# A fused attention and expert-mixture block in split fp32: the mixture's product in two fp32r passes, with the values' read-back issued earlier

## The reference: what is computed

```python
h = layernorm(x) * (1 + ca) + sa
x = x + ga * attention(h)          # 32 heads of 128, 8 KV heads, causal, rope on 64 of 128 dims
h = layernorm(x) * (1 + cb) + sb
# experts' mixture, per token, 64 experts, top 8:
logits = h @ router_weight.T + router_bias
scores = softmax(logits); w, idx = top_k(scores, 8)
w_dense = zeros(T, 64); w_dense[token, idx] = w
out = h * w.sum() + w_dense @ expert_bias      # expert_bias is 64 x 512
x = x + gb * out
```

## Time and profile before

| | |
|---|---|
| median of 3 runs | 1534.45 us (1532.57 to 1534.9) |
| the profiled execution | 1534.65 us |
| its span | 1533.1 us |
| granted TensorE clock, mean | 0.990 |
| VectorE, ScalarE, GpSimd busy | 76%, 64%, 69% |

### The profile page before, as it was taken

One profiled execution on the slowest core, in us unless ns is written; L12 is line 12 of the kernel. 1 busy time (PEld: TensorE's weight loads), 2 busy tenths in 40 slices (PEclk: granted clock), 3 DMA queues, 4 the chain that ended last, 5 costly groups with the idle time before them and its releaser, 6 DMA issues.

```text
span 1533.1 us, 24840 instructions
## 1 busy us (share of the span) xinstructions
PE 1495.0 (98%) x7474; PEld 1260.7 (82%) x7474; DVE 1160.9 (76%) x3433; ACT 975.5 (64%) x2315; POOL 1061.0 (69%) x801
## 2 busy tenths in 40 slices
PE   7979999999999999999999999999999999999987
PEld 4668888888888888888888888888888888888875
DVE  6866777777777777778777777777878888887765
ACT  3346766677666666667667676676656666665673
POOL 1666766776667676667667667666777878876765
PEclk9999999999999999999999999999999999999996
DMA  8547565665656656566565665667678778787760
GB/s 307 212 146 234 193 216 180 202 201 185 213 184 208 202 190 212 181 206 191 194 202 190 211 198 196 202 197 230 204 242 269 258 256 263 250 264 250 242 183 28
DMA packets 210741, 321.62 MB, mean 210 GB/s; under 512 B 38368, under 2 KB 128224, under 8 KB 210608
## 3 DMA queue, kind: packets, MB, share of 16 engines
q1 hardware_dynamic: 210288, 319.94, 65.3%
q10 hardware_dynamic: 320, 0.11, 0.0%
HBM read 179.02 MB, written 140.94 MB: 209 GB/s over the span
## 4 chain that ended last, share of the span: by engine, by line
PE 82%; POOL 5%; DVE 4%; DMA 3%; SPq 2%; issue 2%; ACT 2%; POOLq 0%; DVEq 0%; ACTq 0%
PE bank_s L483 20%; PE bank_o L580 20%; PE bank_pv L565 14%; PE bank_s L530 13%; PE bank_s L506 5%; PE bank_s L494 5%; POOL PT_lo L1424 2%; PE bank_s L462 1%; PE bank_s L598 1%; DMA blocks<-blocks 1%; PE bank_s L610 1%; DMA kv_raw<-vblocks 1%; SPq L1693 1%; SPq L1656 1%; DMA wmod<-in_wmod 1%
## 5 line engine op out<-in xcount | busy, mean ns | idle before, releaser
L1424 POOL TENSOR_TENSOR PT_lo<-PT_raw,PT_hi 128x640 fp32r<-128x640 f32 x252 | 399.3, 1608 | 70.8 <-ACT PT_hi L828 70.6
L814 ACT ACTIVATE probs<-probs,row_inv 128x512 f32<-128x512 f32 (+3 forms) x512 | 258.8, 554 | 178.4 <-DVE row_inv L1105 178.0
L1412 POOL TENSOR_TENSOR rot_c<-rot_c,rot_s 128x512 f32<-128x512 f32 x128 | 165.6, 1294 | 243.5 <-DVE rot_s L1068 243.5
L807 ACT ACTIVATE probs<-probs,row_min 128x512 f32<-128x512 f32 (+3 forms) x512 | 280.6, 552 | 8.7 <-DVE row_min L1099 8.5
L1099 DVE CUSTOM_DVE_ANT_0 probs<-bank_s,mask 128x512 f32<-128x512 f32 (+3 forms) x512 | 231.5, 487 | 1.0 <-issue 0.6
L1417 POOL TENSOR_TENSOR qT_lo<-rot_c,qT_hi 128x512 fp32r<-128x512 f32 x128 | 167.3, 1307 | 92.8 <-ACT qT_hi L789 92.8
L483 PE MATMUL bank_s<-hT_lo,wq_hi 128*128 128x512 f32 x500 | 204.7, 409 | 4.8 <-DVE row_min L1099 2.4
L1122 DVE STREAM_TRANSPOSE blocks<-probs 128x384 f32<-128x384 f32 x508 | 205.2, 442 | 4.1 <-POOL hT_lo L1402 2.1
L580 PE MATMUL bank_o<-wo_lo,OT_hi 128*128 128x512 f32 x504 | 196.6, 390 | 1.8 <-DVE OT_lo L1130 1.8
L580 PE MATMUL bank_o<-wo_hi,OT_hi 128*128 128x512 f32 x504 | 196.3, 389 | 0.0
L580 PE MATMUL bank_o<-wo_hi,OT_lo 128*128 128x512 f32 x504 | 196.3, 389 | 0.0
(11 more groups left out here) (242 smaller groups left out, 3382.9 us busy)
## 6 DMA issues: line engine op xcount, KB each, us to landing
blocks<-blocks SPq DMA_DIRECT2D x127, 640.0 KB, 4.0
PT_raw<-blocks SPq DMA_DIRECT2D x504, 160.0 KB, 3.1
stage<-in_wq SPq DMA_DIRECT2D x32, 256.0 KB, 4.0
vblocks<-kv_raw SPq DMA_DIRECT2D x32, 256.0 KB, 4.3
kv_raw<-vblocks SPq DMA_DIRECT2D x128, 64.0 KB, 3.0
stage<-in_wo SPq DMA_DIRECT2D x32, 256.0 KB, 3.8
split_wq<-wq_hi SPq DMA_DIRECT2D x32, 256.0 KB, 3.9
split_wq<-wq_lo SPq DMA_DIRECT2D x32, 256.0 KB, 4.2
```

What stands on the lines that cost most here:

```text
L807: ins = act.activation(row(t, qt), row(t, qt), ACT.Exp, bias=row_min[m][:, qt:qt + 1], scale=-1.0, accum_out=row_sum[m][:, qt:qt + 1])
L814: ins = act.activation(row(t, qt), row(t, qt), ACT.Copy, scale=row_inv[t % 2][:, qt:qt + 1])
L1412: pool.tensor_tensor(rot_c[:], rot_c[:], rot_s[:], ALU.add).then_inc(pool_a, 1)
L1424: pool.tensor_tensor(lo[:, at], raw_of(t)[:, at], hi[:, at].bitcast(F32), ALU.subtract).then_inc(pool_t, 1)
```

## The change

**The mixture's operands are split.** The expert rows are loaded twice, into partitions 0 to 63 and 64 to 127 of `experts_in`, and are split into `experts[0]` (hi, ScalarE) and `experts[1]` (lo, GpSimd), 128x512 each, at step 96. The weights of a tile become 128x128 in fp32r: columns 0 to 63 hi, 64 to 127 lo. Transposed, they have hi in partitions 0 to 63 and lo below, so that two fp32r matmuls with 128 rows give all four products. GpSimd makes the weights' two parts for the 12 early tiles, in the step after the selection, behind `split_moved_lo`; VectorE makes them for the last 4. For batch 3 the experts are loaded again (SyncE, step 122, after the last early mixture), folded with the gate (GpSimd, step 124), and split again (ScalarE at the end of its step 124, GpSimd in step 125).

**The weights' transpose moves.** It goes from the end of the mixture step to the end of the next step, and from bank s2 to bank s1. The scores' second block now waits for the logits' bias, the third block (256 columns) for the copy of h or of the transposed weights.

**The values' read-back moves.** `load_values` is issued right behind the probabilities' blocks, ahead of the weights' loads and stores.

The diff, cut to its core:

```diff
@@ tensor: scores, ffn_mix, step
                     if qt == 2 and before is not None:
-                        tile_waits((wT_copy, before - 3), last=EARLY_TILES - 1)
+                        tile_waits((bias, before - 2), last=EARLY_TILES - 1)
                     if qt == 1 and before is not None:
                         tile_waits((h2T_copy, before - 1), last=EARLY_TILES - 1)
+                    if qt == 1 and now is not None:
+                        tile_waits((wT_copy, now - 4), last=EARLY_TILES - 1)
...
             def ffn_weights_T(i, ps):
-                    pe.wait_ge(weighed, i + 1)
-                    pe.transpose(bank[ps][0:EXPERTS, 0:P], weight[i % W_RING][:], ident[:]).then_inc(wT, 1)
+                    pe.wait_ge(w_lo, i + 1)
+                    pe.transpose(bank[ps][:, 0:P], weight[i % W_RING][:].bitcast(F32), ident[:]).then_inc(wT, 1)
...
-                    pe.matmul(bank[ps][:], weightT[i % W_RING][:], experts[:], start=True, stop=True).then_inc(
+                    if i in (0, EARLY_TILES):
+                        pe.wait_ge(e_lo, 1 if i == 0 else 2)
+                    pe.matmul(bank[ps][:], weightT[i % W_RING][:], experts[1][:], start=True, stop=False)
+                    pe.matmul(bank[ps][:], weightT[i % W_RING][:], experts[0][:], start=False, stop=True).then_inc(
                         mix_done, 1)
...
                     ffn_transpose(early(n - 1), "s1")
-                    tile_waits((bias, n - 2), last=EARLY_TILES - 1)
-                    ffn_weights_T(early(n - 3), "s2")
+                if before is not None:
+                    pe.wait_ge(dve_s, score_read(t + 1, 0))
+                    ffn_weights_T(early(before - 3), "s1")
@@ scalar
+            def split_experts(n):
+                if n == 0:
+                    act.wait_ge(d_experts, 32)
+                else:
+                    act.wait_ge(folded, 3)
+                act.activation(experts[0][:], experts_in[:], ACT.Copy).then_inc(e_hi, 1)
...
+                if t == FFN_FROM + 5:
+                    split_experts(0)
+                if t == ALL - 4:
+                    split_experts(1)
                 if n is not None:
                     ffn_h2T(early(n - 1), "s1")
-                    ffn_weights_copy(early(n - 3), "s2")
+                if before is not None:
+                    ffn_weights_copy(early(before - 3), "s1")
@@ vector (last four tiles) and gpsimd (early tiles)
+            def ffn_split_weights(i):
...
+                    pool.wait_ge(weighed, i + 1)
...
+                    pool.tensor_copy(weight[w][:, 0:EXPERTS], rest[w][:]).then_inc(w_hi, 1)
+                    pool.wait_ge(w_hi, i + 1)
+                    pool.tensor_tensor(weight[w][:, EXPERTS:], rest[w][:], weight[w][:, 0:EXPERTS].bitcast(F32),
+                                       ALU.subtract).then_inc(w_lo, 1)
@@ gpsimd
             def fold_gate():
-                pool.wait_ge(mix_done, EARLY_TILES)
-                pool.tensor_tensor(experts[:], experts[:], gate[0:EXPERTS, :], ALU.mult).then_inc(folded, 1)
...
+            def fold_experts():
+                pool.wait_ge(d_experts, 64)
+                pool.tensor_tensor(experts_in[:], experts_in[:], gate2[BATCH - 1][:], ALU.mult).then_inc(folded, 1)
...
                     split_moved_lo(t - 1)
+                if before is not None:
+                    ffn_split_weights(early(before - 3))
...
+                if t == FFN_FROM + 5:
+                    split_experts(0)
                 if t == ALL - 6:
                     fold_gate()
+                if t == ALL - 4:
+                    fold_experts()
+                if t == ALL - 3:
+                    split_experts(1)
@@ sync
                 if moved(t):
                     load_transposed(t)
+                if t % GROUP == 3 and t // GROUP + 1 < UNITS:
+                    load_values(t // GROUP + 1)
                 if t >= 1:
                     load_next(t)
...
-                if h == 3 and u + 1 < UNITS:
-                    load_values(u + 1)
...
+                if t == FFN_FROM + 3:
+                    load_experts(0)
+                if t == ALL - 6:
+                    load_experts(1)
```

More of the change, by code:

```diff
@@ L195, in build @@
         after0 = Region(lo_start)
-        experts = after0.take("experts", [EXPERTS, HID])
         router = after0.take("router", [P, CH, EXPERTS])
-        logit, rest, weight = ([after0.take(f"{n}{i}", [P, EXPERTS]) for i in range(W_RING)]
-                               for n in ("logit", "rest", "weight"))
-        weightT = [after0.take(f"weightT{i}", [EXPERTS, P]) for i in range(W_RING)]
+        logit, rest = ([after0.take(f"{n}{i}", [P, EXPERTS]) for i in range(W_RING)] for n in ("logit", "rest"))
+        weight = [after0.take(f"weight{i}", [P, 2 * EXPERTS], F32R) for i in range(W_RING)]
+        weightT = [after0.take(f"weightT{i}", [P, P], F32R) for i in range(W_RING)]
         assert after0.at <= lo_start + hT_bytes
@@ L204, in build @@
         h2 = [(after1 if i < F_RING - 1 else after2).take(f"h2_{i}", [P, HID]) for i in range(F_RING)]
+        experts_in = Region(after2.at).take("experts_in", [P, HID])
+        experts = [after2.take(f"experts_{p}", [P, HID], F32R) for p in ("lo", "hi")][::-1]
+        assert after2.at <= lo_start + 3 * hT_bytes
         gate1, shift2, scale2, gate2 = [], [], [], []
@@ L508, in v_proj, with scores @@
                 mm.then_inc(pe_v, 1)
-            def scores(t, tiles, before=None):
+            def scores(t, tiles, before=None, now=None):
                 if tiles[0] == QUERY_ORDER[0]:
@@ L620, in step @@
                 u, h, n, before = t // GROUP, t % GROUP, ffn_tile(t), ffn_tile(t - 1)
-                scores(t + 1, QUERY_ORDER, before)
+                scores(t + 1, QUERY_ORDER, before, n)
                 if t == 0:
@@ L1208, in ffn_replace @@
                     if i >= W_RING:
-                        dve.wait_ge(weighed, i - W_RING + 1)
+                        dve.wait_ge(w_lo, i - W_RING + 1)
                     dve.match_replace(rest[w][:], top8[i % F_RING][:], logit[w][:], 0.0).then_inc(replaced, 1)
@@ L1456, in add_x, with split_experts @@
                 pool.tensor_tensor(y[:, i, :], y[:, i, :], x_end[j][:], ALU.add).then_inc(residual, 1)
+            def split_experts(n):
+                pool.wait_ge(e_hi, n + 1)
+                pool.tensor_tensor(experts[1][:], experts_in[:], experts[0][:].bitcast(F32), ALU.subtract).then_inc(e_lo, 1)
             def ffn_stats(i):
@@ L1702, in load_rows, with load_router, load_experts @@
                     sp.dma_start(to[:], mod_d[n, b:b + 1, :].broadcast_to([P, HID])).then_inc(d_rows[b], 16)
-            def load_experts():
+            def load_router():
                 sp.wait_ge(pe_qp, GROUP * last_unit(0) + GROUP)
-                sp.dma_start(experts[:], A["eb"]).then_inc(d_router, 16)
                 sp.dma_start(router[:], A["rw"]).then_inc(d_router, 16)
                 sp.dma_start(router_bias[:], A["rb"].broadcast_to([P, EXPERTS])).then_inc(d_router, 16)
+            def load_experts(n):
+                if n == 0:
+                    sp.wait_ge(pe_qp, GROUP * last_unit(SHARED - 1) + GROUP)
+                else:
+                    sp.wait_ge(mix_done, EARLY_TILES)
+                for half in range(2):
+                    sp.dma_start(experts_in[half * EXPERTS:(half + 1) * EXPERTS, :], A["eb"]).then_inc(d_experts, 16)
             def ffn_load(i):
```

36 lines of the change are left out of this document (25 added, 11 removed).

## The result

The changed kernel takes 1529.26 us (median of 12 runs, 1525.66 to 1538.62) against 1535.06 (12 runs, 1532.57 to 1537.62): ratio 0.9964, 95% interval 0.9949 to 0.9979, so 5.5 us faster. The prediction was 1521.5 with a range of 1518.0 to 1528.5: the direction held, the size did not. It was 7.8 us too low, and the median lies 0.8 us above the range. The profiled execution took 1527.11 us with a span of 1525.8, 7.5 and 7.3 us less than before.

The account below looks back on a forecast made before the run. The prediction took TensorE, busy 1495.0 of 1533.1 us, as the bound. Its terms, -8.5 - 2.4 + 0.5 - 3.8 + 0.5 + 1.5 - 0.9, gave -13.1 us from 1534.65: 1521.5 us, range 1518 to 1528.5.

Parts of the forecast that it names:

- Term 7: Last four tiles: two fp32r mixture passes outweigh eight small VectorE operations of 0.25 us each; -0.9 us, bounds +0.5 and -2.
- Term 3: Earlier values' read-back ends ScalarE's wait, removing TensorE stalls in steps 5, 53, 93, 94, 97, 101, 105; -3.8 us.
- Term 1: Twelve early mixtures: output-to-logits distance on TensorE shrinks from 1.37 to 0.69 us with two fp32r matmuls; -8.5 us.
- Term 2: Moved weights' transpose: wait of the scores' second block goes in step 98 and five of nine later steps; -2.4 us.
- Terms 4 and 5: Early tiles: GpSimd's new operations and the experts' split hidden, 0; VectorE held up behind GpSimd by the lock, +0.5 us.
- Term 6: End of step 124: ScalarE waits for GpSimd's fold, output projection starts late; +1.5 us, bounds 0 and 2.8.
- Rival B: Early tiles: each new GpSimd operation holds up VectorE through the port lock; 3.1 us more, 1524.6 us; chance 0.07.
- Rival A: Mixture stretch: VectorE at 91% sets the pace, so removed stalls return under other names; -7.9 us, 1526.7 us; chance 0.2.

Follow-up runs that it names:

- values_only: The kernel before with only the values' read-back moved ahead of the weights' loads; 1532.09 us, ratio 0.9976.
- weights_behind: The changed kernel with SyncE's issue of all the weights moved behind the blocks' store; 1527.31 us, ratio 0.9949 to the kernel before.
- late_copy: The changed kernel with ScalarE's second split of the experts at the end of step 125 in place of 124; 1528.69 us, ratio 0.9952.
- norm_first: The changed kernel with GpSimd's split of the early weights put behind its two operations on h; 1526.55 us, ratio 0.9943.
- tail_fp32: The changed kernel with the last four tiles' mixture in one fp32 matmul again and no second split of the experts; 1528.44 us, ratio 0.9955.
- values_back: The changed kernel with only the values' read-back put back behind the weights' loads; 1538.65 us, ratio 1.0014 to the kernel before.
- dve_split: The changed kernel with the early tiles' split of the weights on VectorE in place of GpSimd; 1541.52 us, ratio 1.0038.

## Why the prediction was wrong

Three steps of the working failed. Term 7 had the sign wrong, because it priced VectorE's new operations at the end without GpSimd's in their way. Term 3 put at nothing what the moved read-back does to the entries behind it in the queue, and counted two stalls that are not its own. And the sum added the terms as if each stood alone, in a stretch where the other engines had little slack left. Term by term:

**Term 1** (-8.5) held in its own steps: 0.68 us from output to logits for 0.69, 8.7 us in the twelve steps. What it left out is that 1.35 us come back, nearly all in the steps between (7.4 net).

**Term 2** (-2.4) held in the five steps at 0.27 each, and the four steps that do not pay were rightly left out. For its step 98 (0.88) it gave 0.13: ScalarE's copy of h, one block later, was late by nearly as much. "Where a stall goes, what is late next" was not asked there, though the step has a second wait on the same engine 0.5 us behind.

**Term 3** (-3.8) was near alone (3.7 measured, 2.9 of it in the five stalls named), and in the changed kernel the move is worth more, 7.7. But two of its parts failed. Steps 93 and 94 (0.9) hardly moved: their waits are not the read-back's. And "what is now issued later by 1.9 us are weights that are first used two or three steps on: nothing" looked at the weights and not at what is queued behind them: the blocks' store, whose way to its read-back grew from 5.5 to 7.2 us in step 99 and from 6.1 to 6.7 in the median. That cost, put at nothing, needs the shorter steps as well: it is absent in `values_only`. Its own share of the missing time is not isolated, since `weights_behind` alone is not resolved.

**Terms 4 and 5** (0, +0.5): GpSimd's two operations measure 0.24 and 0.32 us alone, and cost little where I put them. But the price of the lock was looked for in these new operations only. It acts on old ones, which the shorter steps leave without slack: 0.6 us in step 102.

**Term 6** (+1.5) measured 2.2, 1.9 of them removed by the late copy: mechanism and place right, size within its bounds.

**Term 7** (-0.9) is the largest miss: +0.9. I priced VectorE's new operations at 0.25 us each, although showed an operation of the same size at 1.02 inside a GpSimd operation; here they took up to 1.22. No row stood behind the 0.9 us for two passes at the low clock either: they took 1.22 (1518.25 to 1519.47). Rival B had the mechanism, but I let it act in the early tiles and not at the end, where nothing covers it.

Of the 5.7 us between forecast and table, 1.8 are term 7, 1.6 steps 1, 2, 91 and 92, 0.75 step 98, 0.8 steps 93 and 94, 0.7 term 6, 0.6 step 102; the others came out 0.6 better. On top of it the median is 2.2 us over the profiled execution, where before it was 0.4. The likely source is stalls that differ between executions: the profiles show such stalls in steps 101 to 106 (up to 1.7 us). But no run shows the cause of each slower execution, and the range had no room for them. The profiled execution, at 1527.11, would have been inside the range; what took the median out of it is this scatter, whose cause stays open. Rival A's forecast of 1526.7 was near in time, but mostly by luck: its reason, VectorE's pace, is part of the 1.35 us and of step 102, and the terms 6 and 7, which it kept as forecast, hold 2.5 us of the miss.

## What to carry to other kernels

When an issue moves ahead in a queue, ask what the queue's later entries now stand behind, stores and their read-backs above all, and how soon they follow: that, not the moved transfer, was the price here. When the second and third engines are busy 90% of the stretch, a gain on the leading one takes away their slack: price the terms together, allow for more scatter, and put no work, however small, on the busier of the two, VectorE here. At the end of a kernel, where nothing covers it, price a small VectorE operation as long as the GpSimd operation that it can meet.

## What was not expected of the hardware

The pace of a step can have two levels, 0.57 us apart, by which of two operations of VectorE and GpSimd starts first: 12.7 or 13.3 us in step 102, and likewise in step 106 of `late_copy` and step 114 of `norm_first`. Step 122 has the same two lengths for another reason: in `tail_fp32`, where it took 13.25, VectorE stood 0.39 us for the earlier blocks' DMA. A stall can cost twice. In step 125 TensorE gets from the last scores to the output projection in 2.8 to 3.0 us in five profiles, where 1.1 is the rule in the others; in two of them (`weights_behind`, `norm_first`) the granted clock fell to its lower level (0.50 of 2.4 GHz) around the stall's end and the step took 10.9 and 10.7 us, in the other three (the changed kernel, `values_back`, `dve_split`) it stayed at 1.00 and the step took 9.6 to 9.8. The same fall follows the 1.9 us of step 98 in `dve_split`. Whether a stall costs its own length or 1 us more is different from one execution to the next, one more possible reason for the scatter. And at the end, at a granted clock of 0.50, the fp32 mixture of 64 rows takes 2.07 us against 1.22 us for two fp32r passes of 128 rows (0.59 from start to start, and 0.63 for the second).
